# Attention with a top-2 mixture of experts: six half batches by ordered rows in two groups of three, instead of seven in groups of four and three

## The chip, the core and the metric

One Trainium2 chip, one NeuronCore used. The metric is the device time of one execution in microseconds (us).

## What is computed

The input x is 4 batches of 1024 tokens with 128 features, fp32. One transformer block with the layer norm behind each half:

```python
x = layernorm(x + attention(x))      # 16 heads of 8; K and V through a latent of 32; scores scaled by a decay exp(-1e-4*|i-j|)
logits = x @ w_router                # 8 experts
top_logits, top_idx = top_k(logits, 2); scores = softmax(top_logits)
expert_e(r) = (silu(proj) * gate) @ fc2_w[e],  proj, gate = split(r @ fc1_w[e])
moe = sum over the two chosen experts of scores * expert(x)
shared = silu(x @ gate_w) * (x @ up_w) @ down_w      # inner width 256, every token
out = layernorm(x + moe + shared)
```

## The kernel before

The tokens are cut into eight half batches c = 0..7 of 512 tokens (four tiles of 128). **The first stage** is attention, half batch after half batch, 32 tiles each. TensorE (PE) makes scores (L914), ScalarE (ACT) their exponentials (L776, 512 of them), PE multiplies these with V (L930). Beside the tiles of half batch c, side steps finish attention, norm and routing of half batch c-1.

**The two ways to the experts.** Some half batches are computed *dense*: all eight experts on all 512 tokens, results weighted by a factor that is zero for experts not chosen (`add_down`, L1515). The others go by *ordered rows*: each token's row is sent twice to the place of its expert in a DRAM list (`send`, L609, 8 indirect DMAs by GpSimd (POOL) per half batch), the list is worked off in *units* of four blocks of 128 rows with one expert per block, results are stored to DRAM, and each half batch fetches its two results per token back (`fetch`, L621, 8 indirect DMAs) before VectorE (DVE) combines them (`combine`, L1552). Rows can be sent once the counts of the whole group are known (`order_counts` to `order_experts`, semaphore slots_ready). Before, the groups are half batches 0 to 3 (40 blocks, 10 units) and 4 to 6 (32 blocks, 8 units); only half batch 7 is dense.

**The second stage** runs behind the last attention tile. A list `work` written by hand sets the order for all engines. Each entry is a unit, a `shared` piece (shared expert of one half batch, two pairs of inner columns) or a dense piece (one expert on one half batch). At step k, PE does the transpose of a coming unit's rows (`turn_block`, L856), the two up products of entry k (`up`, L1050 for units, L1055 otherwise), then the down product of entry k-1 (`down`, L1064 unit, L1066 dense, L1068 and L1069 shared). ACT takes the silu (L822), copies turned rows (L812) and unit results (L827) and issues row loads (L793) and result stores (L798); DVE multiplies silu by gate (`hidden`, L1501), adds dense (L1515) and shared results (L1509), and at the steps of `COMBINE_AFTER` runs `combine` and the statistics of the second norm (L1255, L1247, L1250, L1251). All of them share eight PSUM banks as a ring. POOL takes the statistics to the power -0.5 (`ln2_power`, L597, L598), ACT applies them (`rows_out`, L786) and SyncE (SP) stores the half batch (L519). SP also loads the weights of unit u into one of four buffers (`load_weights`, L452, four DMAs of 192 KB) as soon as PE has done unit u-4, and in between the expert numbers into registers (L442). Five steps of half batch 7's attention, norm and routing (`LAST_STEPS`) stand at steps 0, 1, 2, 6 and 8.

```python
shared_before = {0: 0, 4: 1, 10: 2, 12: 3, 14: 4, 16: 5}
COMBINE_AFTER = {18: [0], 21: [1], 23: [2], 26: [3], 29: [4], 33: [5], len(work): [6]}
FINISH_ORDER = list(range(GROUP - 1)) + [LAST, GROUP - 1]
```

`combine_last` (L1563, L1564) is a form of `combine` for half batch 6, tile by tile as its fetches land. A fetch starts when the results of its whole group are stored (`units_stored`) and PE has come to a given place of the ring (`fetch_after`).

Of the kernel before, what the change touches and what calls it, by code (L numbers as in the profile page):

```python
# [27 lines left out]
GROUPS = [(0, 4, 0, 40), (4, 7, 40, 72)]  # L28
# [23 lines left out]
def block_kernel(nc, x, Wq, Wk, Wv, Wo, Wd, Wuk, Wuv, Wr, fc1, fc2, gate_w, up_w, down_w,  # L52
# [4 lines left out]
    F = F2 // 2  # L57
# [30 lines left out]
    with ExitStack() as ctx:  # L88
# [73 lines left out]
        x_blk = [pool_f[:, 0, :], pool_f[:, 1, :], kflat[:, 2 * UB * 3 * F:2 * UB * 3 * F + HALF], kflat[:, 2 * UB * 3 * F + HALF:2 * UB * 3 * F + 2 * HALF]]  # L162
        x_scaled = [osb[:, 0, :], osb[:, 1, :], aT[:, :]]
# [53 lines left out]
        last_gathered = [sem(f"last_gathered{t}") for t in range(CT)]  # L217
# [62 lines left out]
        shared_before = {0: 0, 4: 1, 10: 2, 12: 3, 14: 4, 16: 5}  # L280
        work = []
        for u in range(UNITS):
            if u in shared_before:
                work += [("shared", shared_before[u])]
            work += [("unit", u)]
        work += [("shared", c) for c in range(len(shared_before), GROUP)]
        for c in range(GROUP, NCH):
            work += [("dense", c, e) for e in range(E)] + [("shared", c)]
# [32 lines left out]
        def fetch_after(c, i):  # L321

            n = ring["dn", "unit", (FIRST_UNITS if c < GROUPS[0][1] else UNITS) - 1][0] + (2 * CT * (c % GROUPS[0][1]) + i) * 3 // 2
            k = [k for k, cc in COMBINE_AFTER.items() if c in cc][0]
# [13 lines left out]

        def small_tile(n, *dims):
# [6 lines left out]
        var, rstd, gap, gexp, mhalf, ebase = (small_tile(CT) for _ in range(6))  # L346
# [4 lines left out]
        mv2 = [small_tile(CT * 2, 1) for _ in range(NCH)]  # L351
        var2, rstd2, shift2, w1, w2 = ([small_tile(CT) for _ in range(NCH)] for _ in range(5))
        assert at[0] <= small.shape[1], at[0]
# [44 lines left out]
        def _(sp):  # L398
# [45 lines left out]
            def load_rows(u):  # L444
                sp.dma_start(x_blk[u % AHEAD].rearrange("p (k d) -> p k d", k=UB),
                             sorted_dram[u * HALF:(u + 1) * HALF, :].rearrange("(k p) d -> p k d", p=P)).then_inc(unit_rows_loaded[u % AHEAD], 16)

            def load_weights(u):
                if u >= AHEAD:
                    sp.wait_ge(ring_ready, ring["dn", "unit", u - AHEAD][0])  # L450
                for k in range(UB):
                    sp.dma_start(wblk[u % AHEAD][:, k, :], expert_dram[bass.ds(block_reg[u * UB + k], 1), :, :].rearrange("o p n -> (o p) n")).then_inc(blocks_loaded[u % AHEAD], 16)  # L452
# [1239 lines left out]
```

## Time and profile before

| | us |
|---|---|
| median of 3 runs | 699.66 |
| the three runs | 700.48, 699.66, 695.37 |
| profiled execution, its own time | 696.64 |
| its span in the trace | 694.8 |

The profile is one execution. Engines are shown with their busy time; PEclk is the clock granted to TensorE as a share of 2.4 GHz; a bracket behind a row tells how long the engine had been idle and who released it. PE rows of the timeline count a product's weight loads as instructions too, and their durations overlap, so a step's cost is best read as the difference of the starts of two rows.

### The profile page before, as it was taken

The numbers are of one execution on the slowest core, as the hardware profiler recorded it, in microseconds if no ns is written. First come the engines' busy times: TensorE is split into PE (matmuls) and PEld (weight loads), VectorE is DVE, ScalarE is ACT, GpSimd is POOL, SyncE is SP. The second block draws the span as 40 slices with busy tenths as digits, with TensorE's granted clock in tenths as the row PEclk, the third lists the DMA queues.
The fourth block names the chain that finished last, engine by engine and source line by source line (L and its number), as shares of the span: only waits on it lengthen the run. The fifth ranks groups of instructions, "written<-read, shape, count | busy, mean of one in ns | idle before, by whom it ended". The sixth has DMA issues, their size and how long they took to land.

```text
span 694.8 us, 12833 instructions
## 1 busy us (share of the span) xinstructions
PE 639.3 (92%) x4723; PEld 285.7 (41%) x4723; DVE 305.8 (44%) x972; ACT 546.6 (79%) x638; POOL 292.8 (42%) x281
## 2 busy tenths in 40 slices
PE   4788999999999999999999999999999999999770
PEld 2322333333333333333333332333333787877340
DVE  2552333435344334534463443433345433257773
ACT  2667799999999999999999998999999444334222
POOL 0809551460470056045105624552103640477772
PEclk9999899999999999999999998999999999999975
DMA  5336998355256335625622576432223899874221
GB/s 162 119 123 210 379 391 290 131 186 174 92 197 212 104 118 203 231 92 196 199 77 92 197 255 207 162 109 96 92 78 103 279 286 299 266 252 107 73 77 56
DMA packets 77285, 121.05 MB, mean 174 GB/s; under 512 B 7008, under 2 KB 52512, under 8 KB 77216
## 3 DMA queue, kind: packets, MB, share of 16 engines
q1 hardware_dynamic: 56064, 104.17, 44.8%
q10 hardware_dynamic: 17568, 8.64, 4.3%
q0 software_dynamic: 3584, 7.35, 3.5%
q8 instruction: 40, 0.66, 0.4%
q14 instruction: 29, 0.24, 0.1%
HBM read 71.37 MB, written 50.33 MB: 175 GB/s over the span
## 4 chain that ended last, share of the span: by engine, by line
PE 68%; DMA 9%; DVE 6%; SPq 5%; POOL 4%; ACT 3%; issue 2%; ACTq 0%; POOLq 0%; DVEq 0%
PE ps L930 27%; PE ps L914 18%; DMA queries<-stack_dram 5%; PE ps L1055 5%; PE ps L856 4%; ACT probs L776 3%; PE ps L1050 3%; DMA stack_dram<-stage 2%; SPq L442 2%; PE ps L1064 1%; SPq L452 1%; PE ps L976 1%; PE ps L947 1%; PE ps L979 1%; DVE ps L1381 1%
## 5 line engine op out<-in xcount | busy, mean ns | idle before, releaser
L776 ACT ACTIVATE probs<-ps 128x1024 f32<-128x1024 f32 x512 | 479.9, 1043 | 37.4 <-DVE ps L1381 27.5
L930 PE MATMUL ps<-probs,V 128*18 128x512 f32 x2048 | 273.4, 607 | 0.6 <-ACT probs L776 0.4
L914 PE MATMUL ps<-queries,keys 32*128 32x512 f32 (+3 forms) x1408 | 181.6, 413 | 12.1 <-DMA queries<-stack_dram 6.8
L1381 DVE TENSOR_TENSOR ps<-ps,cpk 128x256 f32<-128x256 f32 x256 | 101.8, 429 | 136.3 <-PE ps L914 135.3
L914 PEld LDWEIGHTS ps<-queries,keys 32*128 32x128 f32 x1408 | 93.0, 186 | 155.0 <-ACT probs L776 95.5
L569 POOL TENSOR_TENSOR stage<-qk,rows_sb 128x512 fp32r<-128x512 f32 x32 | 40.8, 1275 | 133.7 <-DVE qk L1228 128.5
L609 POOL DMA_INDIRECT sorted_dram<-xn,slots x56 | 54.9, 981 | 60.9 <-ACT probs L776 39.1
L822 ACT ACTIVATE probs<-ps 128x512 f32<-128x512 f32 x42 | 25.0, 596 | 47.9 <-PE ps L1055 29.4
L930 PEld LDWEIGHTS ps<-probs,V 128*18 128x18 f32 x2048 | 34.6, 96 | 56.2 <-issue 41.1
L1501 DVE TENSOR_TENSOR probs<-probs,ps 128x512 f32<-128x512 f32 x42 | 28.8, 687 | 50.8 <-PE ps L1055 23.3
L621 POOL DMA_INDIRECT queries<-result_dram,slots x32 | 32.8, 1024 | 29.5 <-PE ps L1050 20.0
L1055 PE MATMUL ps<-xnT,stage 128*128 128x512 f32 x96 | 45.2, 608 | 0.0
L571 POOL TENSOR_TENSOR stage<-pool_f,stage 128x512 fp32r<-128x512 f32 x32 | 40.8, 1274 | 2.5
L570 POOL TENSOR_TENSOR pool_f<-qk,rows_sb 128x512 f32<-128x512 f32 x32 | 40.8, 1277 | 0.0
L602 POOL TENSOR_TENSOR small<-small 128x4 f32<-128x4 f32 x8 | 8.2, 1022 | 60.8 <-DVE small L1277 60.8
L589 POOL TENSOR_TENSOR small<-small 128x4 f32<-128x4 f32 x8 | 8.2, 1027 | 59.2 <-DVE small L1251 59.2
L579 POOL TENSOR_TENSOR squares<-qk 128x512 bf16<-128x512 f32 x16 | 16.3, 1039 | 20.7 <-DVE nmax L1357 11.9
L1055 PEld LDWEIGHTS ps<-xnT,stage 128*128 128x128 f32 x96 | 17.6, 197 | 15.8 <-issue 13.9
L1385 DVE COPY osb<-ps 128x512 f32<-128x512 f32 x16 | 11.1, 692 | 29.0 <-PE ps L930 29.0
L827 ACT ACTIVATE probs<-ps 128x512 f32<-128x512 f32 x14 | 8.4, 597 | 15.6 <-PE ps L1064 15.6
L812 ACT ACTIVATE probs<-ps 128x512 f32<-128x512 f32 x18 | 10.7, 594 | 10.1 <-PE ps L856 10.1
L621 POOL DMA_INDIRECT osb<-result_dram,slots x16 | 16.2, 1012 | 5.5 <-issue 4.1
(187 smaller groups left out, 599.7 us busy)
## 6 DMA issues: line engine op xcount, KB each, us to landing
stack_dram<-stage SPq DMA_DIRECT2D x60, 512.0 KB, 6.5
keys<-stack_dram SPq DMA_DIRECT2D x30, 512.0 KB, 3.7
queries<-stack_dram SPq DMA_DIRECT2D x30, 512.0 KB, 5.8
keys<-stack_dram SPq DMA_DIRECT2D x30, 256.0 KB, 4.7
keys<-expert_dram SPq DMA_DIRECT2D x36, 192.0 KB, 3.4
sorted_dram<-y_pre SPq DMA_DIRECT2D x1, 4608.0 KB, 19.1
rows_sb<-expert_dram SPq DMA_DIRECT2D x20, 192.0 KB
result_dram<-probs ACTq DMA_DIRECT2D x14, 256.0 KB, 4.5
```

What stands on the lines that cost most here:

```text
L569: rest(nc.gpsimd.tensor_tensor(hi, src, tab, ALU.mult))
L570: link(nc.gpsimd.tensor_tensor(pool_f[:, v, :], src, tab, ALU.mult))
L571: rest(nc.gpsimd.tensor_tensor(lo, pool_f[:, v, :], hi.bitcast(F32), ALU.subtract))
L609: pool.indirect_dma_start(out=sorted_dram, out_offset=bass.IndirectOffsetOnAxis(ap=slots[:, s, k:k + 1], axis=0), in_=xn[:, k // CT, tok(k ...
L621: pool.indirect_dma_start(out=gathered[c % GD][:, s, tok(t)], out_offset=None, in_=result_dram[0:rows, :], in_offset=bass.IndirectOffsetOn ...
L776: nc.scalar.activation(probs[:, m % 3, 2 * j:2 * j + 2, :], ps[:, 2 * s:2 * s + 2, :], ACT.Exp, scale=SCALE).then_inc(exp_done, 1)
L856: last = nc.tensor.transpose(dst[:, tok(t)], src[:, tok(t)], ident)
L914: last = mm(bank[2 * s + i][:, lo:hi], keys[rows, u, kt // CT, v, tok(kt % CT)], queries[rows, u, v, lo:hi], start=True, stop=True)
L930: last = mm(bank[OUT_BANK][32 * i:32 * i + 2 * (HD + 1), :], V[:, c // 2 % 2, kt, k + i, half * (HD + 1):(half + 2) * (HD + 1)], probs[:, ...
L1055: last = mm(dst, up_sb[:, e, k * F:(k + 1) * F], xnT[:, c, :], start=True, stop=True)
L1381: tt(d, d, diag_fix.unsqueeze(1).to_broadcast([P, 2, P]), ALU.mult).then_inc(diag_done, 1)
L1501: tt(hid[:, i % 4, :], silu[:, i % 3, :], b, ALU.mult).then_inc(ring_by_dve, 1)
```

## The change

The groups become half batches 0 to 2 and 3 to 5, 32 blocks or 8 units each, so 16 units instead of 18. Half batch 6 is now dense like 7: eight more dense pieces, and no send, fetch or combine for it (48 sends and 48 fetches instead of 56 each). Its first four dense pieces stand between units, the rest behind the last unit; the shared pieces of 3, 4, 5 and 6 come behind the units. The first group's counts are ready a half batch earlier, and so are the second group's: all its sends are now placed beside the attention of half batch 7. Weights of unit 1 and rows of units 2 and 3 get buffers of their own that are free earlier, and are loaded before attention ends. The powers of the second norm are taken for two half batches at a time for the first six.

```diff
-GROUPS = [(0, 4, 0, 40), (4, 7, 40, 72)]
+GROUPS = [(0, 3, 0, 32), (3, 6, 32, 64)]
...
+        w_first = {1: qk[:, :, :, :].rearrange("p a n s -> p (a n s)")[:, 0:UB * 3 * F]}
+        x_first = {2: xT[:, 0, :], 3: xT[:, 1, :]}
...
-        shared_before = {0: 0, 4: 1, 10: 2, 12: 3, 14: 4, 16: 5}
...
+        dense = [[(c, e) for e in range(E)] for c in range(GROUP, NCH)]
+        work = piece("shared", 0) + piece("unit", 0, 1, 2, 3)
+        for u, filler in ((4, piece("dense", dense[0][0])), (6, piece("dense", dense[0][1])), (8, piece("dense", dense[0][2])),
+                          (10, piece("shared", 1)), (12, piece("shared", 2)), (14, piece("dense", dense[0][3]))):
+            work += filler + piece("unit", u, u + 1)
+        work += piece("dense", *dense[0][4:]) + piece("shared", GROUP) + piece("shared", *range(3, GROUP))
+        work += piece("dense", *dense[1]) + piece("shared", LAST)
...
-        COMBINE_AFTER = {18: [0], 21: [1], 23: [2], 26: [3], 29: [4], 33: [5], len(work): [6]}
-        FINISH_ORDER = list(range(GROUP - 1)) + [LAST, GROUP - 1]
-        ROWS_AT = [23, 26, 29, 32] + [len(work)] * 4
+        FINISH_AFTER = {17: 0, 20: 1, 24: 2, 29: 6, 31: 3, 34: 4, 37: 5, len(work): 7}
+        FINISH_ORDER = list(FINISH_AFTER.values())
+        ROWS_AT = [24, 25, 33, 34, 37, 38] + [len(work)] * 2
...
             load_weights(0)
+            sp.wait_ge(side_kept, numbers["v", LAST])
+            load_rows(2)
+            load_rows(3)
+            load_weights(1)
             sp.wait_ge(scores_ready, 2 * TILES)
-            load_weights(1)
-            load_rows(2)
             load_weights(2)
-            load_rows(3)
             sp.wait_ge(pv_done, TILES)
             load_weights(3)
...
+            def ln2_powers(i, n):
+
+                pool.wait_ge(var2_ready, i + n)
+                cols = slice(CT * i, CT * (i + n))
+                means = mv2_all.rearrange("p (c k) -> p c k", k=2)[:, cols, 0]
+                link(nc.gpsimd.tensor_tensor(rstd2_all[:, cols], var2_all[:, cols], mhalf_wide[:, 0:CT * n], ALU.pow))
+                nc.gpsimd.tensor_tensor(shift2_all[:, cols], means, rstd2_all[:, cols], ALU.mult).then_inc(rstd2_ready, n)
...
+                if c == NCH - 1:
+                    pool.wait_ge(slots_ready, 3)
+                    for k in range(12, 15):
+                        send(k, exp_done, 2 * (TPC * c + 4 + 2 * (k - 12)))
...
+                if c == NCH - 1:
+                    for k in range(15, 19):
+                        send(k, exp_done, 2 * (TPC * c + 12 + 2 * (k - 15)))
...
+                if c == NCH - 1:
+                    for k in range(19, 24):
+                        send(k, exp_done, 2 * (TPC * c + 21 + 2 * (k - 19)))
...
-            for k in range(first, GROUP * CT):
-                i = 2 * (k - first)
-                if i < 8:
-                    send(k, exp_done, 2 * (TPC * LAST + 24 + i) if i >= 4 else 0)
-                else:
-                    send(k, ring_ready, (i - 8) * 3 // 2)
...
-                if c:
-                    ln2_power(c - 1)
-            ln2_power(LAST)
+                if c in (2, 4, 5):
+                    ln2_powers({2: 0, 4: 2, 5: 4}[c], 2)
+            ln2_powers(NCH - 2, 1)
...
-            def combine_last(c):
...
-                    if u == FIRST_UNITS + 1:
-                        load_rows(FIRST_UNITS)
-                    if u < UNITS and u != FIRST_UNITS:
+                    if u < UNITS:
                         load_rows(u)
```

In the program, PE's stretch of units 4 to 9 before (L856 turns rows, L1050 and L1064 are a unit's up and down products):

```order
L856 MATMUL ps<-cpk,keys 128x128 x4
L1050 MATMUL ps<-probs,keys 128x128 x8
L1064 MATMUL ps<-keys,probs 128x128 x4
L952 MATMUL ps<-Wr_sb,xnT 128x8 x4
L856 MATMUL ps<-cpk,pool_f 128x128 x4
L1050 MATMUL ps<-probs,V 128x128 x8
L1064 MATMUL ps<-keys,probs 128x128 x4
L856 MATMUL ps<-cpk,pool_f 128x128 x4
L1050 MATMUL ps<-probs,rows_sb 128x128 x8
L1064 MATMUL ps<-V,probs 128x128 x4
L1050 MATMUL ps<-probs,keys 128x128 x8
```

The same place in the changed kernel (L872 turns, L1066 and L1080 are a unit's products, L1071 and L1082 the up and down products of a dense piece):

```order
L872 MATMUL ps<-cpk,keys 128x128 x4
L1066 MATMUL ps<-probs,keys 128x128 x8
L1082 MATMUL ps<-stage,probs 128x128 x4
L1066 MATMUL ps<-probs,V 128x128 x8
L1080 MATMUL ps<-keys,probs 128x128 x4
L872 MATMUL ps<-cpk,pool_f 128x128 x4
L1071 MATMUL ps<-xnT,stage 128x512 x2
L1080 MATMUL ps<-V,probs 128x128 x4
L872 MATMUL ps<-cpk,pool_f 128x128 x4
L1066 MATMUL ps<-probs,rows_sb 128x128 x8
L1082 MATMUL ps<-stage,probs 128x128 x4
```

Every second unit now has a dense piece in front of it, where six units stood in a row.

DVE near the end of the program before, around the combination of half batch 3 (L1552) inside half batch 7's dense pieces (L1501 `hidden`, L1515 the weighted add):

```order
L1501 TENSOR_TENSOR probs<-probs,ps 128x512
L1515 SCALAR_TENSOR_TENSOR qk<-ps,small,xn 128x128 x4
L1552 SCALAR_TENSOR_TENSOR xT<-x_res,small,xT 128x128 x8
L1255 BN_STATS small<-xT 128x6 x4
L1247 BN_AGGR small<-small 128x2 x4
L1250 TENSOR_SCALAR small<-small 128x4
L1251 TENSOR_SCALAR small<-small 128x4
L1501 TENSOR_TENSOR probs<-probs,ps 128x512
```

DVE in the changed kernel, around the combination of half batch 5 (L1565) inside the same dense pieces (L1517 `hidden`, L1531 the weighted add):

```order
L1517 TENSOR_TENSOR probs<-probs,ps 128x512
L1531 SCALAR_TENSOR_TENSOR qk<-ps,small,qk 128x128 x4
L1565 SCALAR_TENSOR_TENSOR qk<-queries,small,qk 128x128 x8
L1271 BN_STATS small<-qk 128x6 x4
L1263 BN_AGGR small<-small 128x2 x4
L1266 TENSOR_SCALAR small<-small 128x4
L1267 TENSOR_SCALAR small<-small 128x4
L1517 TENSOR_TENSOR probs<-probs,ps 128x512
```

The block of one combination with its statistics is unchanged. Before, three of them stand inside half batch 7's dense pieces (3, 4, 5) and one behind them (6); now three stand inside (3, 4, 5), one inside half batch 6's (2), and none behind.

## Rows read from the trace of the kernel before

**Rows 1.** The page's busy times of the engines, whole span.

```profile
PE 639.3 (92%) x4723; PEld 285.7 (41%) x4723; DVE 305.8 (44%) x972; ACT 546.6 (79%) x638; POOL 292.8 (42%) x281
```

**Rows 2.** Busy us by stretch (PE, PEld, DVE, ACT, POOL), PEclk, DMA share, GB/s.

```profile
430.00:470.00 40.00, 39.98 (x318) 14.28 (x314) 14.41 (x41) 39.44 (x44) 21.84 (x23) 1.00 0.43 138
480.00:520.00 40.00, 39.48 (x314) 14.29 (x312) 16.31 (x58) 38.82 (x43) 4.13 (x4) 1.00 0.26 91
540.00:600.00 60.00, 58.78 (x445) 50.99 (x438) 22.04 (x61) 26.19 (x44) 22.00 (x23) 1.00 0.92 286
600.00:640.00 40.00, 40.00 (x269) 32.40 (x268) 23.32 (x73) 16.36 (x30) 30.84 (x33) 1.00 0.68 205
640.00:680.00 40.00, 27.18 (x116) 16.84 (x114) 30.12 (x111) 11.50 (x25) 30.92 (x33) 0.86 0.27 72
```

**Rows 3.** PE's timeline: start us, us, instruction, and idle time before it.

```profile
540.59 0.66 PE L856 MATMUL ps<-cpk,pool_f 128*128 128x128 f32 x4
...
583.35 2.02 PE L1050 MATMUL ps<-probs,keys 128*128 128x128 f32 x16 [0.78 <-DMA keys<-expert_dram]
...
586.10 0.60 PE L856 MATMUL ps<-cpk,keys 128*128 128x128 f32 x4
586.54 3.60 PE L1055 MATMUL ps<-xnT,stage 128*128 128x512 f32 x8
589.97 1.05 PE L1064 MATMUL ps<-keys,probs 128*128 128x128 f32 x8
590.86 0.60 PE L856 MATMUL ps<-cpk,keys 128*128 128x128 f32 x4
591.30 1.95 PE L1050 MATMUL ps<-probs,keys 128*128 128x128 f32 x16
593.09 0.39 PE L1068 MATMUL ps<-stage,probs 128*128 128x128 f32 x2
...
594.87 1.95 PE L1050 MATMUL ps<-probs,V 128*128 128x128 f32 x16
```

**Rows 4.** PE's timeline among the dense pieces of half batch 7.

```profile
644.07 1.05 PE L1066 MATMUL ps<-stage,probs 128*128 128x128 f32 x8
644.96 1.88 PE L1055 MATMUL ps<-xnT,stage 128*128 128x512 f32 x4
648.56 1.13 PE L1066 MATMUL ps<-stage,probs 128*128 128x128 f32 x8 [1.72 <-DVE probs L1501]
649.53 1.88 PE L1055 MATMUL ps<-xnT,stage 128*128 128x512 f32 x4
...
661.17 2.04 PE L1066 MATMUL ps<-stage,probs 128*128 128x128 f32 x8 [4.54 <-DVE probs L1501]
663.01 3.20 PE L1055 MATMUL ps<-xnT,stage 128*128 128x512 f32 x4
666.04 1.06 PE L1066 MATMUL ps<-stage,probs 128*128 128x128 f32 x8
...
673.04 0.39 PE L1069 MATMUL ps<-stage,probs 128*128 128x128 f32 x2
```

**Rows 5.** DVE's timeline: the combination of half batch 3 and the `hidden` behind it.

```profile
643.75 2.31 DVE L1552 SCALAR_TENSOR_TENSOR xT<-x_res,small,xT 128x128 f32<-128x128 f32 x8
...
647.73 0.69 DVE L1501 TENSOR_TENSOR probs<-probs,ps 128x512 f32<-128x512 f32 x1
```

**Rows 6.** POOL's timeline at the end: the last power of -0.5.

```profile
683.78 1.01 POOL L597 TENSOR_TENSOR small<-small 128x4 f32<-128x4 f32 x1 [2.02 <-DVE small L1251]
```

**Rows 7.** ACT's timeline at the end: the last output rows.

```profile
685.10 1.65 ACT L786 ACTIVATE qk<-qk,small 128x128 f32<-128x128 f32 x4 [1.42 <-POOL small L598]
```

**Rows 8.** POOL's timeline: the first and the last of 56 fetches.

```profile
596.96 1.10 POOL L621 DMA_INDIRECT queries<-result_dram,slots  x1 [19.39 <-PE ps L1050]
...
678.10 1.00 POOL L621 DMA_INDIRECT osb<-result_dram,slots  x1 [0.30 <-issue]
```

**Rows 9.** All row sends: duration in ns (min/median/max), first and last start.

```profile
L609 POOL DMA_INDIRECT sorted_dram<-xn,slots x56: 964/969/1226, 407.5 to 564.0; - x56
```

More of the change, by code:

```diff
@@ L279, in block_kernel, with piece @@
         LAST = NCH - 1
-        shared_before = {0: 0, 4: 1, 10: 2, 12: 3, 14: 4, 16: 5}
[L281 to L288, printed above, removed]
+        def piece(kind, *numbers):
+            return [(kind,) + (n if isinstance(n, tuple) else (n,)) for n in numbers]
+        dense = [[(c, e) for e in range(E)] for c in range(GROUP, NCH)]
[5 more added lines that the diff above has]
+        work += piece("dense", *dense[1]) + piece("shared", LAST)
+        assert len(work) == UNITS + NCH + E * (NCH - GROUP) and [w[1] for w in work if w[0] == "unit"] == list(range(UNITS))
         FIRST_UNITS = GROUPS[0][3] // UB
         LAST_STEPS = {0: "o", 1: "a", 2: "wo", 6: "x", 8: "lg"}
-        COMBINE_AFTER = {18: [0], 21: [1], 23: [2], 26: [3], 29: [4], 33: [5], len(work): [6]}
-        FINISH_ORDER = list(range(GROUP - 1)) + [LAST, GROUP - 1]
-        ROWS_AT = [23, 26, 29, 32] + [len(work)] * 4
+        FINISH_AFTER = {17: 0, 20: 1, 24: 2, 29: 6, 31: 3, 34: 4, 37: 5, len(work): 7}
+        FINISH_ORDER = list(FINISH_AFTER.values())
+        ROWS_AT = [24, 25, 33, 34, 37, 38] + [len(work)] * 2
         ring = {}
@@ L345, in block_kernel @@
         mv = small_tile(CT * 2, 1)
-        var, rstd, gap, gexp, mhalf, ebase = (small_tile(CT) for _ in range(6))
+        var, rstd, gap, gexp, ebase = (small_tile(CT) for _ in range(5))
+        mhalf_wide = small_tile(4 * CT)
+        mhalf = mhalf_wide[:, 0:CT]
         logits, top8, idx_f, eq1, eq2 = (small_tile(CT * 8, 1) for _ in range(5))
@@ L1049, in up @@
                     for b in range(UB):
-                        last = mm(dst[:, tok(b)], wblk[u % AHEAD][:, b, k * F:(k + 1) * F], xT_blk[:, u % 2, tok(b)], start=True, stop=True)
+                        last = mm(dst[:, tok(b)], unit_weights(u)[:, b, k * F:(k + 1) * F], xT_blk[:, u % 2, tok(b)], start=True, stop=True)
                 else:
@@ L1581, in _ @@
                     last_step(k)
-                if k == len(work):
-                    dve.wait_ge(ring_by_dve, ring["dn", "shared", LAST][2])
-                    ln2_statistics(LAST)
-                for c in COMBINE_AFTER.get(k, []):
-                    combine(c)
-                    if c != GROUP - 1:
-                        ln2_statistics(c)
+                if k in FINISH_AFTER:
+                    c = FINISH_AFTER[k]
+                    if c < GROUP:
+                        combine(c)
+                    else:
+                        dve.wait_ge(ring_by_dve, ring["dn", "shared", c][2])
+                    ln2_statistics(c)
             dve.wait_ge(side_kept, numbers["flag", 0])
```

57 lines of the change are left out of this document (21 added, 36 removed).

## The prediction

> **What bounds the kernel now.** I read the page first: PE is busy 92% of the span, ACT 79% [rows 1]. The shares by stretch split this in two. In attention ACT is busy 39.4 and 38.8 of 40 us [rows 2], so attention moves at the pace of the exponentials. From 540.6 on PE is the busy one, 58.8 of 60 us at full clock, and DMA comes close with a share of 0.92 at 286 GB/s; from 640 on nobody is full: PE is down to 27 of 40 us, DVE and POOL stand at 30 and 31, and the granted clock is 0.86 on average [rows 2].
>
> PE's timeline of the second stage gives the prices, each the difference of two starts [rows 3]: turning a unit's rows 0.44 us (590.86 to 591.30), a unit's two up products 1.79 (591.30 to 593.09), its down product 0.89 (589.97 to 590.86), a shared piece's up products 3.43 (586.54 to 589.97) and its down products 1.78 (593.09 to 594.87). A dense piece has half of a shared piece's up products, 1.72, and a down product of 0.89 (644.07 to 644.96) [rows 4]. So a unit costs 3.12 us, a shared piece 5.21, a dense piece 2.61. The five steps of half batch 7 come to some 3.0 (two turns and a projection like a down product, a turn, and the routing product at 0.8, an estimate by its place between such rows).
>
> Before: 18 units x 3.12 = 56.2, 8 shared x 5.21 = 41.7, 8 dense x 2.61 = 20.9, steps 3.0, sum 121.8. PE really needs from 540.59 to 673.43 [rows 3, 4], 132.8. The excess of 11.0 is: a wait of 0.78 for weights [rows 3]; a wait of 1.72 for DVE at 648.56, one of 4.54 before 661.17 and half clock behind it, where a down product takes 1.84 instead of 0.89 and two up products 3.03 instead of 1.72, so 2.26 more [rows 4]; and 1.7 in small steps.
>
> Two chains make those waits. DVE works in order, and a combination with its statistics keeps it from 643.75 to 647.73, 3.98 us [rows 5]; the `hidden` behind it comes late and PE's down product waits for that. And POOL fetches without a break from 596.96 to 679.1: 56 fetches, one each 1.475 us with the powers in between (81.14 us by 55) [rows 8]. The fetches of half batch 4 end late, DVE sits in front of its combination and PE gets its 4.54 us. The end then hangs on the last fetches and the last combination. So the second stage has two limits now, PE in its first 100 us and POOL's fetches behind.
>
> **The change, part by part.**
>
> *Arithmetic of PE.* Two units go (6.2 us), eight dense pieces come (20.9): 16 x 3.12 + 41.7 + 16 x 2.61 + 3.0 = 49.9 + 41.7 + 41.8 + 3.0 = 136.4, which is 14.6 more. PE has no room for it: it was busy 98% of the first 60 us. This is the term that costs.
>
> *Fetches.* 48 instead of 56. The first fetch came 7.0 us behind the start of the last unit of its group (589.97 to 596.96) [rows 3, 8]. In the new order unit 15's down product starts behind shared 0 to 2, 16 units, five dense up products, four dense down products and the steps: about 540.6 + 79.0 + 1.7 + 1.7 - 0.9 = 622. The second group's fetches then run from 629 for 24 x 1.475 = 35.4 us to 664. Half batch 3 is fetched by 643 (its 8 fetches and some 2.5 us to land, an estimate), half batch 5 by 667. PE comes to the first dense piece of half batch 7 at about 653 and to the seventh at some 672, so all three combinations in there find their rows landed, by 4 us or more. What goes: the 4.54 us and the 2.26 of half clock. POOL is off the path.
>
> *Combinations on DVE.* The blocks of half batches 3, 4 and 5 stand at steps 31, 34 and 37, in half batch 7's dense pieces, and that of 2 at step 24 in half batch 6's. Each is the case of 648.56: 3.98 us of DVE where a dense piece leaves DVE less than one of slack (0.69 and some 1.12 of work against PE's 2.61). The one clean case cost PE 1.72 [rows 4, 5]. The ends for each are nothing, if the ring of eight banks takes it, and 1.72; I take 1.5, near the row, since the block at step 31 follows a shared piece and has more room. Four make 6.0, with bounds 0 and 6.9. The blocks of 0 and 1 lie in units and shared pieces, as those of 0, 1 and 2 did before, and PE was busy 40.0 of 40 us from 600 to 640 [rows 2]. DVE's added work, eight weighted adds, lies beside PE. The statistics of half batch 6 (1.7 us) stand beside a shared piece of 5.21.
>
> *Weights and rows.* SP's loads of the first units are issued earlier, but PE had no wait there before, so they bring nothing. Unit 9, which waited 0.78, is now reached later by three dense pieces less one shared piece, 7.8 - 5.2 = 2.6 us: that wait goes. A unit moves 768 KB of weights and 256 KB each of rows and results, 1.31 MB, 4.6 us at 286 GB/s. Units 4 to 9 now come with a dense piece to each pair, 8.85 us for two, before six in a row at 3.12; so the demand falls there, and the row sends, which went on until 564 [rows 9], leave the stretch. Between 0 and 5 us for waits on DMA; I take 0.
>
> *Sends.* All of the second group's sends go beside half batch 7's attention. With 23 POOL instructions in 40 us, most of them sends, ACT was as busy as with 4 [rows 2], so I count nothing. A send on POOL takes 0.97 us in the median of 56, from attention at 407 to the tail at 564 [rows 9]. In front of the norm rows of half batch 6 stand six sends on POOL, gated by tile 9 at the latest; the rows are asked for later. The Trainium skill, "DMA: Bandwidth & Descriptors", section on SWDGE, HWDGE and iDMA, says that GpSimd writes descriptors for such DMAs into SBUF, where certain DVE modes lock it out. By that rule sends beside DVE's attention work could take longer; the row's minimum, median and first and last start show no such growth, so the sum is the same by both.
>
> *Small things.* The clearing of the row list is 16 units instead of 18; powers for two half batches at once save POOL some 4 us that nobody waits for. Both nothing.
>
> **Sum.** PE starts the stage at 540.6, works 136.4, and loses 1.7 in small steps as before and 6.0 behind combinations: its last product ends at 684.7. Behind it: 0.8 for DVE's add (0.69 like the other operations on 128x512, and the hand-over), 1.7 for the statistics (3.98 less 2.31) [rows 5], 0.1, then 3.0 from the start of the power to the end of the output rows (683.78 to 686.75) [rows 6, 7], and 8.05 from there to the end of the span (store, and what closes the program). That is 13.7: span 698.4, against 694.8, so 3.6 us more. The profiled execution's own time was 696.64, 1.84 above its span: 700.2 in its terms. The median of the runs is 3.0 above the profiled execution, and 699.66 + 3.6 = 703.3. I forecast 703.
>
> **The rivals.** A measurement can tell about 1% (7 us) from no change.
>
> *A: as summed*, the +14.6 of PE and +6.0 of DVE blocks against 11.0 - 1.7 of stalls and some 8 us of the last combination's tail. 703. Chance 0.60.
>
> *B: the ring takes the combinations.* PE then has no DVE waits: 6.0 less, 697. For it: before, three blocks of combination cost nothing in the units. Against: 648.56 is inside dense pieces, as these are. 0.13.
>
> *C: weights come late, slower.* DMA had a share of 0.92 while PE was nearly full, and the first group's fetches now begin at about 588, 9 us earlier, beside units 8 to 15. If the rate left for units falls from 286 to 250 GB/s, a unit needs 5.2 us; PE takes 5.3 per unit over units 10 to 15 (18.7 + 10.4 + 2.6, by six), but 4.4 over units 4 to 9, so it loses 0.8 on each of these six: 5 us, and up to 8 if the fetches take more, 708 to 711. Weights are four units ahead, so it decides only some way below 286 GB/s, from about 265 by my estimate. Against: the sends have left the stretch. 0.11.
>
> *D: the clock falls at each DVE wait, slower.* Idle of 4.54 us brought half clock, worth 2.26; 1.72 did not, since 648.56 to 649.53 is 0.97 again, near the full-clock 0.89 [rows 4]. If four waits close together did it, 4 x 2.26 = 9.0 more: 712. The Trainium skill, "TensorE: Matmul & The Clock Gate", section "A second HAM failure mode: psum-queue depth-cycling", tells of a kernel whose clock swung with frequent short pauses between groups of products; by that rule this is the outcome. The same page, "Loop structure matters more than you think", lets only long waits do it, and the trace agrees with that one. 0.08.
>
> *E: POOL was the true limit, faster.* If PE hides part of its added work and the end followed the fetches, it would come some 13 us earlier (679 - 664, less the last block moved in), 686. The 98% of PE speaks against. 0.04.
>
> *F: sends slow attention.* If each of the 24 gated sends held a tile up by 0.2 us, 5 us more, 708. 0.04.
>
> **How the numbers follow.** Faster by over 1% (below 692.7): E, 0.04. Slower by over 1% (above 706.7): most of C, D and F, 0.2, and a fringe of A, 0.02: 0.22. The rest 0.74. The range: low, B at 697 with the spread of the runs; high, C at 710. 696 to 710 leaves out D and E and some fringe.
>
> **What would show it.** Right: PE's last product at 683 to 687; waits of PE for DVE's `hidden` of 1 to 2 us at four places, none above 3; the first fetches at about 588 and 629; granted clock 1.0 to the last product; attention over at 540 to 541. Wrong: PE waiting for weights or rows (C), down products of 1.8 us (D), the last combination's fetches ending behind PE (fetch limit), or an attention stage that ends elsewhere than at 540.

## The result, and the profile after

The changed kernel takes 697.18 us (median of 20 runs, 693.86 to 700.13), the kernel before 701.76 (20 runs, 695.37 to 703.87). The ratio is 0.9941, 95% interval 0.9924 to 0.9959: 4.6 us faster by the medians (2.9 to 5.3 by the interval), where 3.6 slower was forecast. The profiled execution took 694.24 us with a span of 692.4.

Busy times of the page and the stretches of the kernel after, as [rows 1, 2]:

```profile
PE 648.8 (94%) x4759; PEld 290.0 (42%) x4759; DVE 313.1 (45%) x999; ACT 547.8 (79%) x640; POOL 274.6 (40%) x259
```

```profile
430.00:470.00 40.00, 39.99 (x322) 14.64 (x318) 16.00 (x60) 39.12 (x43) 16.88 (x17) 1.00 0.36 119
480.00:520.00 40.00, 39.63 (x320) 14.56 (x318) 19.77 (x73) 38.97 (x43) 19.98 (x21) 1.00 0.30 102
540.00:600.00 60.00, 59.50 (x450) 52.17 (x449) 25.87 (x74) 24.76 (x43) 17.04 (x17) 1.00 0.83 258
600.00:640.00 40.00, 38.44 (x226) 28.08 (x225) 27.31 (x91) 15.87 (x30) 26.78 (x28) 1.00 0.41 118
640.00:680.00 40.00, 36.22 (x177) 23.30 (x176) 31.70 (x112) 15.53 (x33) 15.66 (x17) 1.00 0.18 51
```

With 21 POOL instructions beside attention from 480 to 520, ACT is as busy as it was with 4. The clock is 1.00 to the end of PE's work.

PE's timeline of the kernel after, as [rows 3, 4]: the stage's first product, every wait of the stage (there is none before 581), the last product.

```profile
536.68 0.66 PE L872 MATMUL ps<-cpk,pool_f 128*128 128x128 f32 x4
...
581.10 2.02 PE L1066 MATMUL ps<-probs,keys 128*128 128x128 f32 x16 [0.50 <-DMA keys<-expert_dram]
...
626.88 1.13 PE L1082 MATMUL ps<-stage,probs 128*128 128x128 f32 x8 [1.56 <-DVE probs L1517]
...
656.95 1.13 PE L1082 MATMUL ps<-stage,probs 128*128 128x128 f32 x8 [1.12 <-DVE probs L1517]
...
666.57 1.13 PE L1082 MATMUL ps<-stage,probs 128*128 128x128 f32 x8 [1.56 <-DVE probs L1517]
...
678.42 0.46 PE L1084 MATMUL ps<-stage,probs 128*128 128x128 f32 x2 [1.10 <-DVE probs L1517]
...
680.06 0.39 PE L1085 MATMUL ps<-stage,probs 128*128 128x128 f32 x2
```

PE's stage is 143.8 us (536.68 to 680.45), forecast 144.1, with four waits behind combinations of 5.3 us, forecast 6.0. It only starts 3.9 us earlier than in [rows 3].

POOL's and ACT's timelines of the kernel after, as [rows 6 to 8]: the first fetch of each group, the last fetch, the last power, the last output rows.

```profile
583.44 1.13 POOL L640 DMA_INDIRECT queries<-result_dram,slots  x1 [12.93 <-PE ps L1066]
...
622.51 1.13 POOL L640 DMA_INDIRECT x_res<-result_dram,slots  x1 [5.73 <-PE ps L1071]
...
657.04 1.00 POOL L640 DMA_INDIRECT queries<-result_dram,slots  x1 [0.30 <-issue]
...
682.99 1.01 POOL L616 TENSOR_TENSOR small<-small 128x4 f32<-128x4 f32 x1 [6.20 <-DVE small L1267]
```

```profile
684.31 1.65 ACT L804 ACTIVATE qk<-qk,small 128x128 f32<-128x128 f32 x4 [5.84 <-POOL small L617]
```

The last fetch is issued 23 us ahead of PE's last product. From the last output rows (685.96) to the end of the span it is 6.4 us, not the 8.05 of before.

### The profile page after: what moved, and what is told of

It reads as the page before. It is cut to its first block, busy times and chain, and to the rows that moved or that the text cites. A ratio compares the mean times of both kernels' runs of the same rounds, so it can differ in the third digit from the quotient of the medians.

```text
span 692.4 us, 12864 instructions
## 1 busy us (share of the span) xinstructions
PE 648.8 (94%) x4759; PEld 290.0 (42%) x4759; DVE 313.1 (45%) x999; ACT 547.8 (79%) x640; POOL 274.6 (40%) x259
## 4 chain that ended last, share of the span: by engine, by line
PE 71%; DMA 7%; DVE 6%; SPq 5%; ACT 4%; POOL 4%; issue 2%; ACTq 0%; POOLq 0%; DVEq 0%
PE ps L946 27%; PE ps L930 18%; PE ps L1071 6%; PE ps L872 4%; ACT probs L794 4%; DMA queries<-stack_dram 3%; PE ps L1066 2%; DMA stack_dram<-stage 2%; SPq L468 2%; SPq L458 2%; PE ps L995 1%; PE ps L963 1%; PE ps L1082 1%; PE ps L992 1%; PE ps L1080 1%
## 5 line engine op out<-in xcount | busy, mean ns | idle before, releaser
L838 ACT ACTIVATE probs<-ps 128x512 f32<-128x512 f32 x48 | 28.7, 597 | 58.4 <-PE ps L1071 40.0
L628 POOL DMA_INDIRECT sorted_dram<-xn,slots x48 | 47.1, 981 | 62.1 <-ACT probs L794 60.7
L1071 PE MATMUL ps<-xnT,stage 128*128 128x512 f32 x128 | 58.9, 593 | 0.0
L1517 DVE TENSOR_TENSOR probs<-probs,ps 128x512 f32<-128x512 f32 x48 | 32.9, 687 | 45.9 <-PE ps L1071 24.7
L1071 PEld LDWEIGHTS ps<-xnT,stage 128*128 128x128 f32 x128 | 22.5, 191 | 19.1 <-issue 17.9
L1082 PE MATMUL ps<-stage,probs 128*128 128x128 f32 x128 | 17.2, 277 | 4.2 <-DVE probs L1517 4.2
L1082 PEld LDWEIGHTS ps<-stage,probs 128*128 128x128 f32 x128 | 16.2, 191 | 11.1 <-issue 10.5
L1244 DVE COPY qk<-ps 128x512 f32<-128x512 f32 x14 | 9.6, 688 | 18.7 <-PE ps L992 11.9
```

The source lines that it names most:

```text
L628: pool.indirect_dma_start(out=sorted_dram, out_offset=bass.IndirectOffsetOnAxis(ap=slots[:, s, k:k + 1], axis=0), in_=xn[:, k // CT, tok(k ...
L1071: last = mm(dst, up_sb[:, e, k * F:(k + 1) * F], xnT[:, c, :], start=True, stop=True)
L1082: last = mm(dst[:, tok(t)], hids[0][:, tok(t)], dn_sb[:, w[2], :], start=True, stop=True)
L1517: tt(hid[:, i % 4, :], silu[:, i % 3, :], b, ALU.mult).then_inc(ring_by_dve, 1)
```

## The experiments

The times are told as ratios to the kernel before, run on the same chip. Chips differ. The kernel before takes 701.8 us in the first measurement, and 700.8 to 700.9 on the chip of after_third, no_first_fetch, late_fetch, late_sends, before_tile, no_preload, split_blocks and split_spread. It takes 714.5 on the chip of before_again, after_again, late_weights and spread_blocks, 713.5 on that of light_after, light_before, packed_units and late_order, and 713.2 on that of before_third and packed_again. On each of these last three chips all kernels have a stop of PE that is told of at the end. The changed kernel without an edit was run on the first of the three only (after_again). "The stage" is PE's work from its first product behind attention to its last.

**The same kernels again.** before_again and before_third are the kernel before, after_again and after_third the changed one, with no edit.

> The kernel before once more, for a second profile of it. If attention's 4 us (end at 540.6 before, 536.7 after in the first profiles) is made by the change, attention ends here at 540 to 541 again. If it is made by what differs from one execution to the next (the granted clock behind the wait at 412), it ends anywhere from 536 to 543, and the stretch from 416 to 424 shows another clock than 0.56 and 0.59. The second stage from attention's end to the last product: 133 us in either case.

> The changed kernel once more, for a second profile and the ratio again: 0.992 to 0.996 of the kernel before. The stage from attention's end to the last product: 143 to 144 us, with waits of PE for DVE of 1 to 1.6 us at four places. If the change makes attention shorter: end at 536 to 537. If the execution decides: 536 to 541.

> The changed kernel a third time, as the control of this set and a further profile. Expected: 0.988 to 0.994 of the kernel before; a stop of PE (one product per 0.7 us) for some 6 us about 9 us behind the first fetch if this execution has it, as the last eight profiles have; second stage 143.5 us without it, 149 to 152 with it.

> The kernel before a third time. Theory: its first profile was one of its fastest runs; a typical one waits 2 to 5 us for weights at units 8 and 9 and comes to its last product 135 to 138 us behind attention's end. Rival: 133 us with 0.8 of waits, as in the first; then the time between it and the changed kernel is in attention alone.

Measured: after_again 0.9878 (0.984 to 0.9916) on a chip with the stop, after_third 0.9942 (0.9913 to 0.9972) on one without. after_third's attention ends at 537.5 and its PE stage is 143.6 us, with the same four waits (1.56, 1.12, 1.55, 1.10). So the stage is reproducible, and the stop (after_again: 151.4 us) is no part of the change. before_again's second stage took 143.5 us and before_third's 147.0: the 132.8 of [rows 3, 4] is the shortest seen. The expectations for these two had no stop in them and missed, as did after_again's for its ratio and its stage.

What attention is made of shows in DVE's 16 evacuations of the output, one per quad of heads. Their distances agree within some 0.03 us between executions wherever nothing disturbs one, so a fixed change is told from a passing one. DVE's timeline of the kernel before, at the quad that ends near 386:

```profile
353.79 0.69 DVE L1385 COPY osb<-ps 128x512 f32<-128x512 f32 x1 [1.54 <-PE ps L930]
354.40 0.28 DVE L1325 TENSOR_TENSOR room<-small,cpk 128x128 f32<-128x128 f32 x1
...
355.85 0.69 DVE L1228 COPY xT<-ps 128x512 f32<-128x512 f32 x1
...
386.43 0.69 DVE L1385 COPY osb<-ps 128x512 f32<-128x512 f32 x1 [1.98 <-PE ps L930]
```

The same quad in the kernel after:

```profile
354.42 0.69 DVE L1401 COPY osb<-ps 128x512 f32<-128x512 f32 x1 [2.48 <-PE ps L946]
355.03 0.68 DVE L1244 COPY xT<-ps 128x512 f32<-128x512 f32 x1
...
385.73 0.69 DVE L1401 COPY osb<-ps 128x512 f32<-128x512 f32 x1 [1.99 <-PE ps L946]
```

Before, six small steps of order_blocks (354.40 to 355.85) stand behind the evacuation, and then the copy of `xT`; after, the copy stands right behind it. PE and ACT of the kernel before, at the same place:

```profile
356.60 0.66 PE L856 MATMUL ps<-cpk,osb 128*128 128x128 f32 x4 [0.93 <-DVE xT L1228]
```

```profile
357.79 1.94 ACT L776 ACTIVATE probs<-ps 128x1024 f32<-128x1024 f32 x2 [1.07 <-PE ps L914]
```

PE's turn waits for that copy, the scores behind it come late, and ACT stands still. This quad takes 32.65 us in all four profiles of before's code as it was or with lighter loads, and 31.31 in the 15 profiles of the changed kernel and its variants. There the first group has three half batches and its steps come a half batch and a tile earlier (in late_order, below, only the tile). The other fixed differences: the last quad 29.24 against 28.58, two others 0.14 and 0.24 the other way; what makes these three was not traced. In sum attention is 1.6 us shorter. The rest of the 3.9 us is, but for 0.4 of passing differences, a spell at the half clock (1.2 GHz) from 416 to 424, worth 2.7 us in two quads. The stretch in the kernel before and in the kernel after (0.57 and 1.00 are the granted clock):

```profile
416.00:424.00 8.00, 7.75 (x50) 2.32 (x48) 3.01 (x7) 5.26 (x7) 2.74 (x3) 0.57 1.04 336
```

```profile
416.00:424.00 8.00, 7.99 (x66) 2.80 (x68) 4.93 (x19) 7.87 (x10) 3.84 (x4) 1.00 1.02 328
```

Three of five profiles with before's attention have it, none of the 15 others. Ahead of it PE waits for the queries in both kernels, 1.35 us before and 1.19 after. Other such spells (from 160 and from 288) come with either kernel.

**before_tile**, the fixed part tried in the kernel before:

```diff
-                    if step == 1:
+                    if step == 2:
                         order_blocks(c0, c1)
```

> The kernel before, with DVE's step that lays out the blocks (order_blocks) one tile later, behind the copy of xT at the turn of half batch and not ahead of it. Theory: ahead of it, 1.5 us of small DVE steps hold the copy, PE's turn of the output and the next scores, and ACT stands still for 1.07 us at 357.8; so the quad that ends at 386 takes 32.6 us. Then here that quad takes 31.3 to 31.5 and the kernel is 1.0 to 1.5 us faster than before (0.998 to 0.9985). Rival (the 1.3 us are the clock or a transfer): 32.6 as before. Its second stage is that of before: if its profile shows 138 us or more up to the last product where the first profile of before showed 133, the missing gain of the change is there.

Measured: 0.9986 (0.9954 to 1.0018), the quad 31.81 instead of 32.65, and no wait of ACT for PE there; 0.8 of the 1.3 us, where the theory had all of it. Of the rest, 0.45 is a wait of ACT for DVE at 361.1, behind the moved steps. The interval alone would not show it; the quad does. Its second stage had what the first profile of before lacked. PE's timeline of before_tile:

```profile
581.59 2.02 PE L1050 MATMUL ps<-probs,rows_sb 128*128 128x128 f32 x16 [1.44 <-DMA rows_sb<-expert_dram]
...
587.71 2.54 PE L1050 MATMUL ps<-probs,keys 128*128 128x128 f32 x12 [3.20 <-DMA keys<-expert_dram]
```

4.6 us of waits for the weights of units 8 and 9, where [rows 3] had 0.78. PE's stage is 136.4 us, 3.5 more.

**late_order**, the first group's ordering one half batch later in the changed kernel (`step` reduced by TPC for c0 == 0).

> After, with DVE's steps that order the first group's rows one half batch later, at the place where they stood before (half batch 4's end). Read in attention alone. Theory: these steps there cost ACT 1.3 us in the quad from 354 on and save 0.5 from 261 to 292, so attention ends 0.8 us later than in after: the quad that ends at about 387 takes 32.6 us instead of 31.3. Rival (that difference comes from something else): 31.3 as in after.

Measured: 31.30 us for that quad, so my theory of the place falls in this form. One tile decides: here order_blocks runs a tile ahead of the turn of half batch (351.5 to 352.8), in before right at it (354.4 to 355.8). Attention ended at 536.2.

**late_weights**, the loads of the dense experts' weights moved from 413 us to 427 and 442.

> After, with the loads of the dense experts' and shared weights moved from half batch 5's last quad (413 us) to half batch 6's first two (427 and 442). Theory: they compete with the load of the queries that PE waits for at 412, and the clock falls behind that wait in some executions. Then PE's wait there shrinks from 1.2 to below 0.5 us, the clock behind it stays at 1.00, and the median falls by 1 to 3 us against after. Rival: the queries come late because they are issued behind the stores of the parts (398.7 to 407), not because of the weights. Then the wait stays at 1.2 us and the time within 0.5 us of after.

Measured: 0.9873 (0.983 to 0.9917), as after_again, and PE's wait at 415 still 1.24 us. So it is not the weights. That the queries come behind the stores of the parts, as the rival says, fits the order of issue, but was not tried.

**light_after and light_before**, the unit weights cut to a third:

```diff
-unit_weights(u)[:, k, :], expert_dram[..., :, :]
+unit_weights(u)[:, k, 0:(3 if u < AHEAD else 1) * F], expert_dram[..., :, 0:(3 if u < AHEAD else 1) * F]
```

> After, with the loads of the expert weights of units 4 to 15 cut to a third: only the first 128 of the 384 columns are loaded, the other two thirds of each block keep old data (so the outputs of the experts by ordered rows are not the reference's). Count and order of the transfers stay. Theory: in some executions all engines stand still for some 6 us at about 595 to 602, in steps of single products 0.7 us apart, because their code comes by DMA behind the data while the DMA share is near 0.9. Then with the lower share the stop goes, and the median falls by 4 to 6 us against the changed kernel (to 0.980 of before). Rival (the code is late whatever the load): the stop stays, and the time is within 1 us of after's.

> Before, with the loads of the expert weights of units 4 to 17 cut to a third in the same way (the outputs of the experts by ordered rows are not the reference's). Theory: the kernel before has more of these stops and waits for weights than the changed one, 8 to 12 us, so it falls further: 0.983 to 0.988 of before, and then light_before is as fast as light_after or up to 3 us faster (as the sum without them says). Rival (the gain of the change is in attention and in the sum of PE): light_before stays behind light_after by the same 5 to 9 us.

Measured: 0.9898 (0.9851 to 0.9945) and 0.9951 (0.992 to 0.9982). The DMA share from 580 to 600 fell from 0.93 (after_again) to 0.66 in light_after, and the stop stayed where it was, some 5 us long. My theory of it falls. light_before ran 2.6 us behind light_after on the same chip: neither as fast, as the theory had it, nor 5 to 9 us behind, as the rival did, and its 0.9951 misses the 0.983 to 0.988. The lighter weights helped before (0.5%; its wait for them is 0.82 us). That they did not help after is read across chips, 0.9898 here beside after_again's 0.9878.

**packed_units and packed_again**, half batch 6's dense pieces behind the units, shared pieces in their place (units 4 to 9 in a row):

```diff
-        for u, filler in ((4, piece("dense", dense[0][0])), (6, piece("dense", dense[0][1])), (8, piece("dense", dense[0][2])),
-                          (10, piece("shared", 1)), (12, piece("shared", 2)), (14, piece("dense", dense[0][3]))):
+        for u, filler in ((4, piece("shared", 1)), (6, []), (8, []), (10, piece("shared", 2)), (12, piece("shared", 3)), (14, piece("shared", 4))):
```

> After, with half batch 6's dense pieces all behind the units: shared pieces 1 to 4 stand between the units as in the kernel before (ahead of units 4, 10, 12, 14), units 4 to 9 in a row. The work is the same. Theory (dense pieces between the units thin out the transfers and shorten the waits for weights and for code): slower than after by 2 to 4 us. Rival (where the pieces stand costs nothing): within 1 us of after.

> After with units 4 to 9 in a row and shared pieces 1 to 4 in place of the four dense pieces between units. Theory: waits for weights of 2 to 5 us at units 8 and 9, where after has 0 to 0.7, and 1 us more behind combinations; 0.998 to 1.001 of before, 3 to 5 us slower than after. Rival (it was the chip): 0.993 to 0.996 as after.

Measured: 0.9975 (0.9945 to 1.0005) and 0.9953 (0.9915 to 0.9991), beside after_again's 0.9878 on a third chip, which would be 5 to 7 us. On its own chip packed_units, at 710.2, is 2.8 us behind light_after and 4.1 behind the single run of late_order, so the size is uncertain. PE's timeline of packed_units at unit 9:

```profile
588.24 3.65 PE L1065 MATMUL ps<-probs,keys 128*128 128x128 f32 x16 [2.97 <-DMA keys<-expert_dram]
```

The waits for weights are 3.0 and 3.3 us, with the clock lower behind them (0.57 from 588 to 592), and those behind the combinations 6.8 to 7.1 instead of 5.4. The twelve profiles of kernels that have dense pieces between the units and load the full weights show waits for them of 0 to 1.2. So these pieces, which I had given 0 to 5 us and taken at nothing, keep the weights nearly in time; the work is the same in both orders.

**no_preload**, rows 2 and 3 and weights 1 loaded behind attention as before.

> After, with rows 2 and 3 and weights 1 loaded behind the last scores again, into the usual buffers. Theory (PE had no wait at the first units before, so the earlier loads bring nothing): within 1 us of after, 0.993 to 0.996 of before. Rival (the loads stand ahead of units 1 to 3, and the ones behind them come later, where the DMA share is 0.9): waits for weights of 1 to 3 us at units 1 to 9.

Measured: 0.9938 (0.9903 to 0.9973), as after (0.9942 on the same chip). PE had no wait at the first units. The preloads are worth nothing that these runs can tell.

**late_sends**, the second group's sends in POOL's old place:

```diff
-                if c == NCH - 1:
-                    pool.wait_ge(slots_ready, 3)
-                    for k in range(12, 15):
-                        send(k, exp_done, 2 * (TPC * c + 4 + 2 * (k - 12)))
...
+            pool.wait_ge(slots_ready, 3)
+            for k in range(12, 24):
+                i = 2 * (k - 12)
+                if i < 8:
+                    send(k, exp_done, 2 * (TPC * LAST + 24 + i) if i >= 4 else 0)
+                else:
+                    send(k, ring_ready, (i - 8) * 3 // 2)
```

> After with the second group's sends behind POOL's other work of attention, as in the kernel before (8 from about 524, 16 in the first 25 us of the second stage). Theory F extended to sends: PE and DVE stop once in attention's last 10 us or in the first 25 us of the second stage, as in the profiles of before on these chips (533 to 537, 562), and the time is 2 to 6 us above the control. Rival (sends cost nothing where they stand, as the sum had it): within 1 us of the control.

Measured: 1.0047 (1.0019 to 1.0074), 7.3 us above after_third on the same chip. Neither text foresaw how. POOL, ACT and PE of late_sends:

```profile
564.09 0.97 POOL L628 DMA_INDIRECT sorted_dram<-xn,slots  x1 [0.30 <-issue]
```

```profile
567.88 0.38 ACTq L809 DMA_DIRECT2D pool_f<-sorted_dram  x1
...
568.92 0.60 ACT L836 ACTIVATE probs<-ps 128x512 f32<-128x512 f32 x1 [8.38 <-issue]
```

```profile
570.44 2.04 PE L1080 MATMUL ps<-stage,probs 128*128 128x128 f32 x8 [5.75 <-DVE probs L1515]
```

Unit 8's rows wait in ACT's order for the last send (564.09, landed by 567.9), and every `silu` behind it waits too: 5.75 us of PE, and half clock behind (0.51 from 570 to 576; 2.04 for a product of 1.05). With 8 units in the first group this load comes two units earlier than with 10. That the sends cost nothing beside attention shows in the quads: with the second group's sends out of half batch 7's attention, its last three quads take 30.20, 30.49 and 28.58 us, and 30.21, 30.50 and 28.57 in after. So the early sends are free and, in this order of work, needed. The kernel before also held back the row load of the second group's first unit by one unit; late_sends does not, so whether 3 and 3 could do with late sends and that delay is open.

**no_first_fetch and late_fetch**, against the stop:

> After without the first group's 24 fetches and without the wait for them (half batches 0 to 2 are combined from old data, so their outputs are not the reference's). Theory F (the stop of PE at 595 to 602 comes with POOL's indirect fetches: it began 8 to 10 us behind the first of them in all eight profiles): no stop at 590 to 620, PE's stage is 144 to 146 us and the time 5 to 7 us below the control. Rival P (the stop belongs to a place in PE's own program, where its code comes late whatever POOL does): the stop stays at 595, behind the first product of unit 7's or 8's up products, and the time is within 1.5 us of the control.

> After with the first fetch held back until unit 11's down product (about 602 instead of 586), and the combinations of half batches 0, 1, 2 at steps 20, 24, 28. Theory F: the stop moves with the fetches, to 610 or later, and is shorter if dense pieces run there. Rival P: it stays at 595. The time is worth less here, since the later combinations make PE wait: between the control less 4 and plus 6 us.

Measured: 0.9913 (0.9878 to 0.9947) and 1.0122 (1.0088 to 1.0156). They fell on a chip without the stop, so they say nothing about it. PE's stage without 24 fetches was 144.4 us, as after's: PE does not feel them. The 2.2 us by which no_first_fetch beats after_third stand in its profile behind PE's last product (10.1 us to the end of the span instead of 12.0); why was not traced. late_fetch made PE wait 3.9 and 8.4 us for rows and is 12 us above after_third, outside the 6 that were allowed.

**spread_blocks, split_blocks, split_spread**, against the four waits behind combinations. First the whole blocks moved next to shared pieces; then each block cut in three steps (first four weighted adds, other four, statistics); then both.

```diff
-        FINISH_AFTER = {17: 0, 20: 1, 24: 2, 29: 6, 31: 3, 34: 4, 37: 5, len(work): 7}
+        FINISH_AFTER = {17: 0, 20: 1, 25: 2, 29: 6, 30: 3, 33: 4, 36: 5, len(work): 7}
...
-                if k in FINISH_AFTER:
+                for k0, c in FINISH_AFTER.items():
+                    if c < GROUP and k - k0 in (0, 1):
+                        combine(c, k - k0)
+                    if k - k0 == (2 if c < GROUP else 0):
...
                         ln2_statistics(c)
```

> After, with the combinations of half batches 2 to 5 moved next to shared pieces: the shared pieces 4 and 5 stand between half batch 7's dense pieces, and each combination starts one step ahead of a shared piece. Theory (a combination's 4 us of DVE fit behind a shared piece's 3.4 us of up products, not behind a dense piece's 1.7): the four waits of 5.3 us in all fall below 1.5, and the kernel is 3.5 to 5 us faster than after, 690 to 692 in the median. Rival (PE is held by the ring of banks or by the fetches, and the waits only move): within 1.5 us of after.

> After, with each combination cut in three parts (1.2, 1.2 and 1.7 us) behind three steps in a row in place of one block of 4 us. Theory: PE runs 4.33 us ahead of a dense piece's down product (1.72 + 0.89 + 1.72), DVE needs 0.69 + 0.3 for the add before, 3.98 and 0.69, 5.9 in all, so PE waits 1.56; parts of at most 1.7 us fit. The waits at half batch 6 and 7 fall from 5.3 us to 1.5 to 3 (in half batch 7's dense pieces DVE has 28 us of work for 26 of PE's), and the kernel is 2 to 4 us faster than after: 0.989 to 0.991 of before. Rival (the waits are the work of DVE, not its blocks): within 1 us of after.

> The same cut, with shared pieces 4 and 5 between half batch 7's dense pieces as in spread_blocks, so that DVE has 36 us of work for 42 of PE's from shared piece 3 on, and with the last combination done ahead of the last piece. Theory: no wait of PE above 0.7 us is left, PE's stage is 138.5 to 139.5 us, 4 to 5 us faster than after: 0.986 to 0.988 of before. Rival (spread_blocks was slower for another reason than its blocks): slower than after again.

Measured: spread_blocks 0.9959 (0.9926 to 0.9991) beside after_again's 0.9878 on the same chip, so some 6 us slower; split_blocks 0.9895 (0.9841 to 0.9949), 692.5 us, and split_spread 0.9864 (0.9815 to 0.9912), 691.4 us, the fastest of all, beside after_third's 696.2 on the same chip. PE's timeline at the end of spread_blocks, and of split_spread:

```profile
693.91 0.46 PE L1084 MATMUL ps<-stage,probs 128*128 128x128 f32 x2 [2.16 <-DVE probs L1517]
...
696.38 0.63 PE L1085 MATMUL ps<-stage,probs 128*128 128x128 f32 x2
```

```profile
676.64 0.46 PE L1084 MATMUL ps<-stage,probs 128*128 128x128 f32 x2 [0.17 <-DVE probs L1517]
...
678.28 0.39 PE L1085 MATMUL ps<-stage,probs 128*128 128x128 f32 x2
```

A whole block stops PE beside shared pieces too (waits of 7.5 us in sum, 5.4 in after_again), since a shared piece's down product needs two `hidden` from behind the block, and ahead of the last piece nothing is left to run meanwhile; behind the last wait the clock is 0.61 (694 to 697). The waits are 2 of the 5.4 us by which its stage is longer; the rest, part of it a longer stop, was not split up. Cut in parts, the waits fell from 5.3 us to 0.5 and to 0.2, and PE's stage to 138.5 and 138.3 us. The waits were the length of one block of DVE's work, not its sum.

## Why the prediction was wrong

The sum had the arithmetic and the waits of the second stage right. It failed in two terms that it put at nothing: the change in attention, and the waits for weights that the kernel before has in most executions and the changed one does not. A tail summed too long adds to it.

Against the span of 698.4 that I summed, the profiled execution has 692.4. The 6.0 us: attention 3.9, the tail 1.7, PE's stage 0.3. The other 2.2 of the 8.2 us between forecast and medians is told under "from profile to median".

- *Arithmetic of PE, +14.6, and 1.7 of small steps*: right. The stage without the waits behind combinations is 138.4 us against 138.1.
- *Combinations on DVE, 6.0*: right, 5.3; the row at 648.56 carried over. Rival B (the ring takes them) is wrong. The fourth wait came at the last shared piece.
- *Fetches*: right: first fetches 46.8 and 85.8 us behind the stage's start, forecast 47 and 88, POOL off the path, the 4.54 and 2.26 gone. The last rows were fetched over 10 us ahead of their combination. In two variants, late_order and light_after, the wait behind half batch 4's combination is 3.3 and 2.7 us instead of 1.6, though the last fetch of its rows was issued 18 us or more ahead; there DVE came late to the block by 1.1 to 1.7 us, and why was not traced.
- *Attention over at 540 to 541*: the step that failed. I counted sends and order steps there as nothing. The sends are nothing; the order steps stood in the way at one turn of half batch, in a quad that is 1.33 us longer, with a wait of ACT that the timeline of before shows at 357.8 and that I did not look for (before_tile gives back 0.84 of it). With the other fixed differences it is 1.6; the other 2.3 are a spell of half clock in the profile of before, less 0.4 of passing differences.
- *The tail, 13.7*: mis-sized, 12.0. The 8.05 from the last rows to the end of the span is 6.4 now.
- *Weights and rows, "between 0 and 5; I take 0"*: the step that failed in the medians. I took the 0.78 of one execution as the price. Profiles of the kernel before show 0.8, 1.9, 3.1 and (before_tile) 4.6 us; those with dense pieces between the units 0 to 1.2, and packed_units and packed_again, without them, 3.0 and 3.3. Rival C had the sign wrong.
- *Rival D*: wrong. Four waits of 1.1 to 1.6 us, and the granted clock is 1.00, the 2.4 GHz level, from 540 to 680. By the rule of the Trainium skill, "TensorE: Matmul & The Clock Gate", "A second HAM failure mode: psum-queue depth-cycling", it could have fallen; the trace does not show it. Waits of 5.75 (late_sends) and 8.4 us (late_fetch) did bring half clock, and so did one of 2.97 for weights (packed_units); one of 3.9 (late_fetch, at 617.9) did not. Rivals E and F are wrong: PE ran to the end, and the sends did not slow ACT (the quads of late_sends).
- *From profile to median*: I added 3.0 us for both. After's median is 2.9 above its profiled execution, that of before, now from 20 runs instead of 3, is 5.1 above its own: its profile was one of its fast executions, with 0.78 us of waits for weights.

My estimate for the 4.6 us: 1.6 fixed in attention, 1 to 2 from the half-clock spell at 416 (2.7 us in three of five), and the rest in the second stage with the end, 155.1 to 155.7 us in three profiles (after, after_third, no_preload) against 154.2 (first profile) and 158.6 (before_tile). The last part rests on two profiles of before's code without the stop. That the spell belongs to before's attention is counted, not explained.

## What to carry to other kernels

Before a move is priced at nothing in a stage bound by one engine, list that engine's own waits there: a 1 us wait of the bound engine is worth more than twenty hidden instructions. Price the baseline from several executions, since one profile can lack the waits (here up to 4 us for weights) that the change removes. And cut long blocks of a helper engine so that each fits in the leader's lead; here this was worth 3.7 us, and 4.7 with the shared pieces moved as well.

## What the hardware showed that was not expected

On three of the chips used, PE stops in the second stage in a pattern of its own. PE's timeline of after_again:

```profile
595.81 0.28 PE L1066 MATMUL ps<-probs,V 128*128 128x128 f32 x1
596.85 0.39 PE L1066 MATMUL ps<-probs,V 128*128 128x128 f32 x2 [0.76 <-issue]
598.27 0.27 PE L1066 MATMUL ps<-probs,V 128*128 128x128 f32 x1 [1.03 <-issue]
598.99 0.27 PE L1066 MATMUL ps<-probs,V 128*128 128x128 f32 x1 [0.45 <-issue]
599.70 0.48 PE L1066 MATMUL ps<-probs,V 128*128 128x128 f32 x2 [0.44 <-issue]
601.15 2.26 PE L1066 MATMUL ps<-probs,V 128*128 128x128 f32 x9 [0.97 <-issue]
```

One product in 0.7 us, or two, instead of one in 0.11, for some 5 us, with no wait that the profile knows; behind it the clock is lower (0.66 from 601 to 606). The changed kernel and its variants had it there between 593 and 608 us, at the products of unit 11 or right behind them (two variants once more, at 616 and 630), and none had it on the other chips. The kernel before had it starting at 562 to 568, at 611 to 623 and at 642 to 654, and in its three profiles on those chips attention's last quad took 31.6 to 35.0 us instead of 29.24. PE's timeline of before_third in that quad:

```profile
543.56 0.79 PE L914 MATMUL ps<-queries,keys 32*128 32x384 f32 x4 [3.51 <-ACT probs L776]
```

On the one of these chips where the changed kernel ran, the change gains 1.2%, against 0.6% elsewhere. The longer last quads (by 2.3 to 5.7 us) and the several stops of before fit this, but no run takes them away. The stop is not made by the DMA share (light_after). A late supply of code is my guess: the page has a queue of its own for it, 40 packets with 0.66 MB in after's. The Trainium skill, "Runtime: NRT & Kernel Launch", "Instruction fetch mechanics", says that fetching code is hidden behind the pace of issue; no run here decides it, and the cause stays open.
